# The latent layers' scores from whole fp32 queries and keys, one pass in place of three

## The reference

```
B, P, K, H, NH = (4, 512, 64, 512, 16); DH = H // NH        # here B is 16, P and K are 128
h = jnp.concatenate([x, latents], axis=1)
q = (latents @ q_w + q_b).reshape(b, k_len, NH, DH)
kv = (h @ kv_w + kv_b).reshape(b, p + k_len, NH, DH, 2)
kmat, v = (kv[..., 0], kv[..., 1])
attn = jnp.einsum('bkhd,bnhd->bhkn', q, kmat) / DH
attn = jnp.where(full_mask[:, None, None, :], attn, -jnp.inf)
attn = jax.nn.softmax(attn.astype(jnp.float32), axis=-1).astype(q.dtype)
attn_out = jnp.einsum('bhkn,bnhd->bkhd', attn, v).reshape(b, k_len, H)
```

## Time and profile before

| | us |
|---|---|
| median of 3 runs | 2565.93 (2564.32 to 2566.09) |
| the profiled execution, its own time | 2566.45 |
| its span | 2564.5 |
| TensorE busy with matmuls | 2450.6 (96% of the span) |
| VectorE busy | 1235.5 (48%) |
| GpSimd busy | 1118.6 (44%) |
| ScalarE busy | 1085.5 (42%) |

### The profile page before, as it was taken

The page is one execution under the profiler, slowest core; times in us unless marked ns, Lnnn a source line. Parts: engine busy times, 40 slices in busy tenths (PEclk is TensorE's granted clock), DMA queues, the critical chain, the costliest instruction groups (busy, mean ns, idle before and its releaser), DMA issues.

```text
span 2564.5 us, 48767 instructions
## 1 busy us (share of the span) xinstructions
PE 2450.6 (96%) x18464; PEld 2052.2 (80%) x18464; DVE 1235.5 (48%) x3296; ACT 1085.5 (42%) x3712; POOL 1118.6 (44%) x1972
## 2 busy tenths in 40 slices
PE   7999998999999999998888999999999999899999
PEld 6888786888888878886777788888888888788887
DVE  4555655333234666766666442333455555432332
ACT  4555555111113777787676211111555555311111
POOL 2444435600043787878876740023344443730000
PEclk9999999999999999998998999999999999999999
DMA  4111222311034223223453320122022111320100
GB/s 162 59 59 59 96 63 67 95 50 50 1 98 136 74 106 120 90 102 124 137 168 120 116 96 1 50 84 77 26 84 66 51 42 59 116 87 1 50 33 17
DMA packets 106774, 198.07 MB, mean 77 GB/s; under 512 B 8304, under 2 KB 35632, under 8 KB 103600
## 3 DMA queue, kind: packets, MB, share of 16 engines
q1 hardware_dynamic: 106544, 194.97, 22.8%
HBM read 136.22 MB, written 58.72 MB: 76 GB/s over the span
## 4 chain that ended last, share of the span: by engine, by line
PE 79%; ACT 11%; DVE 5%; POOL 3%; issue 1%; DMA 1%; SPq 0%; DVEq 0%; POOLq 0%
PE banks L326 70%; ACT plain_high L731 5%; PE banks L467 5%; PE banks L497 3%; ACT plain_low L731 2%; POOL plain_high L1344 2%; ACT plain_work L796 1%; DVE stats L1135 1%; PE banks L521 1%; DVE rounded_work L1109 1%; ACT plain_work L715 1%; DMA plain_high<-attention_w 0%; DVE plain_work L1150 0%; DVE plain_high L1004 0%; ACT plain_low L715 0%
## 5 line engine op out<-in xcount | busy, mean ns | idle before, releaser
L326 PE MATMUL banks<-rounded_work,rounded_low 128*128 128x512 f32 (+1 forms) x2688 | 536.8, 356 | 18.9 <-DVE rounded_low L1168 9.5
L326 PEld LDWEIGHTS banks<-rounded_work,rounded_low 128*128 128x128 f32 x2688 | 447.4, 200 | 84.4 <-issue 12.3
L982 ACT ACTIVATE plain_work<-banks,columns 128x512 f32<-128x512 f32 x192 | 132.4, 690 | 870.8 <-PE banks L326 870.8
L326 PE MATMUL banks<-rounded_work,rounded_high 128*128 128x512 f32 (+1 forms) x2400 | 480.9, 354 | 1.0 <-DMA rounded_work<-ctx_split 0.6
L326 PEld LDWEIGHTS banks<-rounded_work,rounded_high 128*128 128x128 f32 x2400 | 394.3, 190 | 66.7 <-issue 5.8
L1344 POOL TENSOR_SCALAR plain_high<-plain_high,inv_sum 128x128 f32<-128x128 f32 (+1 forms) x768 | 296.1, 408 | 324.2 <-DVE inv_sum L1026 323.8
L1320 DVE CAST rounded_work<-plain_work 128x512 fp32r<-128x512 f32 x192 | 105.7, 551 | 683.2 <-ACT plain_work L982 672.5
L326 PE MATMUL banks<-rounded_low,rounded_work 128*128 128x512 f32 x1728 | 414.9, 391 | 0.0
L326 PE MATMUL banks<-rounded_high,rounded_work 128*128 128x512 f32 (+1 forms) x1728 | 390.2, 377 | 0.0
L326 PEld LDWEIGHTS banks<-rounded_low,rounded_work 128*128 128x128 f32 x1728 | 321.6, 188 | 68.6 <-issue 2.8
L326 PEld LDWEIGHTS banks<-rounded_high,rounded_work 128*128 128x128 f32 x1728 | 309.1, 188 | 60.6 <-issue 1.4
(11 more groups left out here) (106 smaller groups left out, 3120.6 us busy)
## 6 DMA issues: line engine op xcount, KB each, us to landing
plain_work<-x SPq DMA_DIRECT2D x96, 256.0 KB, 3.2
plain_work<-mlp_w SPq DMA_DIRECT2D x96, 256.0 KB, 2.7
rounded_work<-ctx_split SPq DMA_DIRECT2D x16, 1024.0 KB, 6.0
u<-plain_work SPq DMA_DIRECT2D x48, 256.0 KB, 2.7
plain_work<-u SPq DMA_DIRECT2D x12, 1024.0 KB, 7.1
x<-plain_work SPq DMA_DIRECT2D x48, 256.0 KB, 2.3
plain_work<-attention_w SPq DMA_DIRECT2D x44, 256.0 KB, 2.7
ctx_split<-rounded_work SPq DMA_DIRECT2D x8, 1024.0 KB, 5.6
```

The source lines that it names most:

```text
L326: mm = pe.matmul(dst, lhs(i), rhs(j), start=first and n == 0, stop=last and n == 2, skip_group_check=True)
L982: act.activation(gelu[:, j % 2, :], bank(key), ACT.Gelu_apprx_tanh, bias=col(y, 28 + j)).then_inc(evac_of(key), 1)
```

## The change

The latent layers' keys and queries are kept whole, as plain fp32: `full_keys` (8 KB a partition, from 16 KB on) and `full_queries` (4 KB, from 48 KB on) take the places of `KT_L` and of the latent use of `QT`. ScalarE writes them as before, now without rounding, and counts up the bank's `evacuated` semaphore itself. VectorE's two low-part instructions are left out in these layers. `pe_scores` issues one matmul of plain fp32 operands in place of three of fp32r. The grouped-query and the cross layer keep their split.

```diff
-        KT_L = work(rounded, 16, 2, 4, 4 * P)
...
+        full_keys, full_queries = work(plain, 16, 4, 4 * P), work(plain, 48, 4, 2 * P)
...
                     if y.kind == LATENT:
-                        key_t = lambda h: KT_L[part, h, c, :].rearrange("p (x b n) -> p x b n", x=2, b=2)[:, :, b, :]
-                    elif y.kind == GQA:
+                        pe.matmul(PS[:, r, i * width:(i + 1) * width].rearrange("p (x n) -> p x n", x=2),
+                                  full_queries[part, c, b * P:(b + 1) * P],
+                                  full_keys[part, c, :].rearrange("p (x b n) -> p x b n", x=2, b=2)[:, :, b, :],
+                                  start=i == 0, stop=False, skip_group_check=True)
+                        continue
+                    if y.kind == GQA:
...
             if y.kind == LATENT:
-                act.activation(KT_L[:, 0, i, :], bank(key), ACT.Identity, bias=col(y, 4 + i)).then_inc(hi_done, hi_count(key))
+                act.activation(full_keys[:, i, :], bank(key), ACT.Identity, bias=col(y, 4 + i)).then_inc(evac_of(key), 1)
...
-                last = act.activation(QT[:, 0, t, :], bank(key)[:, j * 256:j * 256 + 256], ACT.Identity, bias=col(y, t))
-            last.then_inc(hi_done, hi_count(key))
+                to = full_queries[:, t, :] if y.kind == LATENT else QT[:, 0, t, :]
+                last = act.activation(to, bank(key)[:, j * 256:j * 256 + 256], ACT.Identity, bias=col(y, t))
+            if y.kind == LATENT:
+                last.then_inc(evac_of(key), 1)
+            else:
+                last.then_inc(hi_done, hi_count(key))
...
         def dve_keys(dve, y, p, i):
+            if y.kind == LATENT:
+                return
             key = ("K", y.n, p, i)
             wait_hi(dve, key)
-            if y.kind == LATENT:
-                dve.scalar_tensor_tensor(out=KT_L[:, 1, i, :], in0=bank(key), scalar=col(y, 4 + i), in1=KT_L[:, 0, i, :].bitcast(F32),
-                                         op0=ALU.add, op1=ALU.subtract).then_inc(evac_of(key), 1)
-            elif y.kind == GQA:
+            if y.kind == GQA:
...
         def dve_queries(dve, y, p, i):
+            if y.kind == LATENT:
+                return
```

## The result

The changed kernel takes 2569.49 us (median of 18 runs, 2566.27 to 2571.91) against 2565.32 us of the kernel before (18 runs, 2560.88 to 2570.57). The ratio is 1.0016, with a 95% interval of 1.0009 to 1.0023: +4.2 us. The interval is clear of 1, so the change costs time, though less than the 5.1 us (0.2%) that the forecast set as the bound of a difference. The forecast was +6.0 us and 2571.9 us, with a range of 2567 to 2579.

A forecast was written before the change was run, and what follows sets the result against it. TensorE, 96% busy, was taken as the bound. Scores +11.2, first pairs -2.0 and -1.0, clock -1.5 and last pairs -0.7 made +6.0 us on 2565.93: 2571.9 us, range 2567 to 2579.

The forecast's parts named there:

- What bounds the kernel: TensorE, busy 96% of the span, decides; VectorE's relief counts only where TensorE waits for VectorE.
- The score term, +11.2 us: Latent scores: four steps of 0.219 us replace six of 0.117, +0.175 us a round over 64 rounds, +11.2 us.
- The estimate of +15 us: Score term by the skill's four-pass rule: 4/3 of the passes, 0.70 us of steps become 0.94, about +15 us.
- the faster rival: Scores: a record is bounded by its weights, not its stream; 0.58 us a round, 2546 us in all; 8%.
- The first pairs, -2.0 and -1.0 us: First scores of layers 0 and 3: ScalarE's end releases them in place of VectorE's, -2.0 and -1.0 us.
- The clock, -1.5 us: Layer 0 behind the first wait: the half clock from 24.4 to 27.8 us goes, -1.5 us, two chances in three.
- The last pairs, -0.7 us: Last pairs of layers 0 and 3: four longer rounds hide ahead of waits for GpSimd's scaling, -0.7 us.
- VectorE, 109 us less busy: Low parts: 64 of keys and 128 of queries leave VectorE, 109 us of work, bringing nothing where TensorE doesn't wait.
- The sum: Whole kernel: +11.2 - 2.0 - 1.0 - 1.5 - 0.7 = +6.0 us, giving 2571.9 us, 0.23% slower.
- no measurable change: Whole kernel: steps of 0.213 make +4.5, one clock dip less +3, 2569 us, under the 5.1 us bound; 28%.
- The rivals: Scores to mask: weight-bound 0.58 us (8%), row groups not all side by side 1.86 (6%), overlap keeping its ratio 1.08 (5%).

The follow-up runs named there:

- the passes alone: Changed kernel, but VectorE still computes a low part that nothing reads and frees the bank: 2574.11 us, ratio 1.0035 to the kernel before.
- the two kernels with a whole cross layer: Kernel before with whole fp32 in the cross layer plus first latent pairs (2553.70 us, 0.9955) or all latent pairs (2561.06 us, 0.9982).
- one fp32r pass: Kernel before with latent low parts left out and only the high parts' product made, 8 matmuls a round: 2534.50 us, ratio 0.9871.
- the relief alone: Kernel before without latent low parts, ScalarE freeing banks, still 24 fp32r matmuls a round from high parts: 2564.68 us (1.0000), again 2564.89 us (0.9994).
- the second one of before: Second profile of the kernel before, run once more with nothing edited: 2565.74 us, ratio 0.9995.
- the kernel with the cross layer only: Kernel before with queries and keys kept whole in plain fp32 in the cross layer, latent layers left as before: 2556.92 us, ratio 0.9967.
- the repeat: The changed kernel measured again on another chip, against the kernel before: 2569.32 us, ratio 1.0015.

## Why the prediction was right, and where its steps were off

**What bounds the kernel.** As read: 0.14 us more a round on TensorE came out at the end nearly in full by the medians (the passes alone, the two kernels with a whole cross layer), and 0.47 us less did too (one fp32r pass).

**The score term, +11.2 us.** The mechanism is as told: two records for a matmul, four steps a round, side by side in four row groups. That a record makes two passes under one weight load is inferred from its time; the trace shows one weight load a record, and no passes. The size was off. The forecast took 0.219 us a step, from the fp32 row with its 128 columns, and had 0.213 as its lower bound. The measured step is 0.214 to 0.216. That the two come so close is partly luck. The value product, from which 0.219 was doubled, has 128 columns, and the cross layer shows that a score step with 128 columns takes 0.11 us in either type and with 64 columns no less: a floor, and no measure of the stream. Whether the value product's 0.109 is such a floor or its stream, no run here shows. Also, the transposes now follow the mask 0.02 us closer (0.22 for 0.24). From the start of the scores to that of the transposes are 1.19 us after and 1.05 before: +0.14, 64 times +9.0 us. The passes alone measured +8.7. The estimate of +15 us that the forecast worked out from the four passes of the Trainium skill ("FP8 and Floating Point Precision", section "TensorE Precision Notes") is refuted as a price, not as a count: a plain fp32 matmul is two records, but a record costs 0.214 us and not twice the 0.117 of an fp32r matmul, so four passes cost 3.7 and not 4. The step from which the faster rival would no longer have saved time is 0.175, (0.81 - 0.11)/4, for the 0.17 told there.

**The first pairs, -2.0 and -1.0 us.** The waits shrank from 3.03 to 1.02 and from 2.04 to 1.13: -2.0 and -0.9, released by ScalarE as told.

**The clock, -1.5 us.** The stretch at half clock is gone, and the first value product of layer 0 starts at 47.17 us for 50.68:

```profile
47.17 1.09 PE L501 MATMUL banks<-plain_high,plain_work 128*32 128x128 f32 x32 [2.23 <-DVE plain_high L1021]
```

That is -3.5, with two longer rounds in it, so -3.8; but 0.2 of it lies ahead of the wait (TensorE runs dry at 20.36 us before and at 20.14 after), which leaves -3.6 for wait and clock where the sum had -3.5. The row that the step rested on, full clock after 2.04 us of idleness in layer 3, was the exception among four profiles; a wait of 1.0 to 1.1 us was followed by full clock at both places in the kernel after and in the relief alone.

**The last pairs, -0.7 us.** Four rounds were to be longer at no cost, and now at 0.14 each that is -0.6. The last pair of layer 3 in the kernel after, TensorE's value product and then GpSimd's scaling, in order of time:

```profile
2176.33 1.08 PE L501 MATMUL banks<-plain_low,plain_work 128*32 128x128 f32 x32
...
2188.17 3.65 POOL L1353 TENSOR_SCALAR plain_low<-plain_low,inv_sum 128x256 f32<-128x256 f32 x8
```

The same two in the kernel before:

```profile
2174.45 1.08 PE L497 MATMUL banks<-plain_low,plain_work 128*32 128x128 f32 x32
...
2186.27 3.65 POOL L1344 TENSOR_SCALAR plain_low<-plain_low,inv_sum 128x256 f32<-128x256 f32 x8
```

Both are 1.9 us later, so the two longer groups between them added nothing: hidden, as told. What holds GpSimd up there, in both, is the arrival of a weight tile by DMA (3.27 and 3.31 us of idleness, ended at 2182.42 and 2184.33), and the wait of TensorE that follows starts from there.

**VectorE, 109 us less busy.** It is 75.3. This was a misreading of a row: line 1080 makes the queries' low parts of every layer, and of its 128 instructions in the earlier trace rows only 64 are the latent layers'. The page of after has 128 VectorE instructions fewer, 64 and 64, and 64 x 0.751 + 64 x 0.476 = 78.5 us, of which neighbours that overlap leave 75.3 in the busy time. VectorE's work in all other layers stayed, as the 64 that are left show (line, operation, shapes, count, busy us, mean ns, and the idle time before them):

```profile
L1089 DVE SCALAR_TENSOR_TENSOR rounded_work<-banks,columns,rounded_work 128x256 fp32r<-128x256 f32 x64 | 27.8, 477 | 8.1 <-ACT rounded_work L776 8.1
```

It cost the forecast nothing, because the term was beside TensorE's work, but the sign that it named to look for was wrong by a third.

**The sum.** Measured piece by piece: +9.0 - 3.6 - 0.9 - 0.6 = +3.9 us, and +4.2 in the medians. The forecast's +6.0 is 2 us too high, nearly all of it the score term. The forecast time, 2571.9, is 2.4 too high: the kernel before was 0.6 us faster in its 18 runs than in the three that the forecast had. By the forecast's own bound of 5.1 us the outcome is its case "no measurable change", to which it gave 28%; that it is slower after all shows only in the interval of 18 runs. The rivals fell by one and the same number: 0.97 us from the scores to the mask, for 0.58, 1.86 and 1.08.

**What stays open.** The relief alone should have been 4.5 us faster and was 0.7 and 0.9 faster, in two runs on two chips, whose intervals end at -2.3 and -3.8 us. Its trace has the gain up to 47 us and keeps most of it to layer 0's end. It loses it in the first pair of the grouped-query layer. TensorE of the relief alone at three waits there:

```profile
803.20 1.65 PE L326 MATMUL banks<-rounded_work 32*128 32x256 f32 x24 [1.89 <-issue]
831.52 2.93 PE L326 MATMUL banks<-rounded_work,rounded_high 128*128 128x256 f32 x12 [1.92 <-DMA rounded_work<-ctx_split]
862.00 0.63 PE L470 MATMUL banks<-ident,plain_high 128*128 128x128 f32 x4 [0.76 <-POOL plain_high L1354]
```

The same three in the kernel before:

```profile
806.16 1.00 PE L326 MATMUL banks<-rounded_work 32*128 32x256 f32 x24 [1.89 <-issue]
832.54 2.93 PE L326 MATMUL banks<-rounded_work,rounded_high 128*128 128x256 f32 x12 [0.61 <-DMA rounded_work<-ctx_split]
862.27 0.63 PE L467 MATMUL banks<-ident,plain_high 128*128 128x128 f32 x4 [0.71 <-POOL plain_high L1344]
```

A lead of 3.0 us shrinks to 1.0 and to 0.3. In the relief's second profile, against the second one of before, 3.2 us (802.48 for 805.68) shrink to 0.5 (859.54 for 859.99). Two things are seen to take it: slower scores at the entry of the layer, and a longer wait for a DMA (1.92 and 1.46 us for 0.61). The first goes with a lower granted clock. The relief alone, a stretch of time:

```profile
798.00:809.00 11.00, 9.12 (x80) 8.72 (x79) 5.23 (x36) 5.50 (x22) 0.00 (x0) 0.84 0.30 99
```

The same stretch in the kernel before:

```profile
798.00:809.00 11.00, 9.11 (x85) 8.49 (x84) 6.29 (x25) 3.12 (x10) 0.00 (x0) 1.00 0.42 145
```

And in the kernel with the cross layer only:

```profile
798.00:809.00 11.00, 9.11 (x75) 8.44 (x75) 5.83 (x25) 3.01 (x10) 0.00 (x0) 0.86 0.46 145
```

The second profile of the relief alone, from the other chip, has 0.84 there too, the changed kernel 1.00. But the cross-layer kernel, whose work up to there is that of before, has 0.86, so the dip at this place isn't the relief's own; it costs 1.5 us (from the wait of 1.89 us to the next, of 1.83 us, are 25.3 us in these three profiles, and 23.8 in both profiles of before and in the changed kernel). The longer wait for the DMA doesn't set the relief apart either: it is 1.45 us in the changed kernel. Why the relief alone should meet the two on average isn't shown.

Nor is it shown that the parts don't add. The medians give -0.7 to -0.9 us for the relief and +8.7 for the passes, 7.8 to 8.0 together, where the change measures +4.2 and +3.5. But a relief of about -2 us and scores of about +6 lie inside every one of the intervals. The changed kernel's own +4.2 us is not in doubt; its split between scores and relief is uncertain by some 3.5 us, between +8.7 and -4.5 and +4.4 and -0.9 (which make the +3.5 of the repeat).

## What to carry to other kernels

Count a score product in TensorE's steps, not in matmuls. With 32 rows and 128 columns a step is at a floor of 0.11 us here, and plain fp32 with its two records beats three fp32r matmuls (cross layer, 0.41 us a group); with 256 columns a step takes longer than the floor (four of 0.214 us against six of 0.117), and the split wins by 0.14 us a round. Remove a conversion where TensorE waits for it, here the first pair of a layer and the grouped-query layer, and leave it where it lies beside TensorE's work. And when a row's count is taken into a sum, ask which layers it comes from.

## What the runs showed of the hardware

- Row groups work side by side only in some orders. With two or three records of the same 32 rows in a row, 16 or 24 of them take 0.97 or 0.81 us, four row groups at a time; with eight in a row, 64 short ones take 4.4 us, 2.5 times what steps of 0.11 in fours would give, two row groups at a time. Not expected; the run as a whole lost 13% to it and to the lower clock that came with it.
- A record of 32 rows and 128 columns of weights takes 0.11 us at least: for 64 and 128 columns moving in plain fp32 and for 128 in fp32r. That the weights set this floor isn't shown; the value product has 32 columns of weights and a step of 0.109 too.
- The half-clock stretches of one and the same kernel differ from execution to execution: a wait of 2.04 us was followed by a granted clock of 1.00 in one profile and 0.91 (over 20 us) in the next. Single traces of this kernel can't carry a claim below 2 us.
